# The first group's block in another order, with the second group's input products moved ahead of the first gate product

## The chip, the cores and the metric

The kernel runs on one core of a Trainium2 chip. The metric is the device time of one execution in microseconds (us); the median of several executions counts. TensorE (PE in the profile, PEld its weight loads), VectorE (DVE), ScalarE (ACT) and GpSimd (POOL) each work through their own instruction list in order; SyncE (SP) issues the DMAs. They meet only at semaphores: `then_inc` on the producer, `wait_ge` on the consumer.

## What is computed

Input: 2048 rows of 512 numbers (8 sequences of 256), float32.

```python
x = x + layernorm(attn(layernorm(x)))     # attn: rmsnorm -> mamba2 -> residual -> rmsnorm -> SwiGLU MLP
x = x + layernorm(ffn(layernorm(x)))      # ffn: linear 512x512 + LoRA of the one expert chosen by argmax
# mamba2(h), per sequence, chunks of 128:
z, xBC, dt = split(h @ w_in.T)            # 512 + 768 + 4 columns
xBC = silu(conv4(xBC) + conv_b); dt = softplus(dt + dt_bias)
Y = (att * exp-decay) @ (x*dt) + C @ state + D * xs
out = (Y * silu(z)) @ w_out.T
```

The SwiGLU MLP has an inner width of 1792, that is 14 blocks of 128.

## The kernel before

A **group** is one sequence (256 rows, two tiles of 128); there are 8. Each goes through three stages: A (both norms and mamba2), B (the MLP, 14 blocks f = 0..13) and C (the ffn). `steps` runs step t = 1..9 with A on group t, B on group t-1, C on group t-2. Within a step every engine has a hand-written table (`A_AT`, `NEXT_AT`, `C_AT`) that says after which block f it does which part of A and C. Group 0's stage A has no step to lie in: it is written out in a function `first()` of each engine. This is the head.

Matrices are multiplied as float16 pairs: each weight unit of 128 x 512 is split into an upper half (`upper_halves`, ACT, line 596) and a lower half (`lower_halves`, DVE, line 919), in place in the ring `W`: unit u is written where the raw of unit u-4 lay, so ACT waits for DVE's split of u-4. A product is then three matmuls for each pair of halves. The scale of the split comes from the largest norm of a matrix, for which PE multiplies every raw block by itself (`grams`, bf16), DVE takes the maximum and writes a diagonal (`prep_diag`), PE spreads it with a matmul (`spread`), and DVE makes the scale (`prep_scale`, `prep_inverse`). There are three such chains: 0 for w_in, 1 for gate and up, 2 for down and the ffn's linear. In the head units 0 to 9 (w_in), 10 to 17 (gate and up of f = 0..3) and 18 (down of f = 0) are split; the rest is split in step 1, three units ahead of each f, by `prepare(f)`, first on ACT, then on DVE.

Stage A, in the order of its data: `a_stats` (mean and variance, DVE), `a_norm` (powers, POOL), `a_center` and `a_hi1`/`a_lo1` (float16 pair of the normalised rows, DVE, ACT, DVE; group 0 uses `first_norm`), `a_t1` (transpose to `ht`: for group 0 on PE with ACT and DVE making the halves, for later groups two transposing DMAs), `a_in(g, b)` for three pairs of w_in units (24 matmuls each) and `a_z(g, b)` for two, `a_dt` (PE, then softplus on ACT with two table loads and ten small DVE operations), `a_conv` (ACT tap, three DVE passes of two operations), `a_silu`, `a_scan_in` and `a_tdt` (POOL, lines 468 and 476), `a_dec` (float32 products, exp on ACT, times dt on DVE), `a_tok` (transposes), `a_att`, `a_xd` (D times xs, POOL line 484, four operations), `a_xw`, `a_ce`, `a_state`, `a_y`, `a_o`, `a_h1`, then `a_sumsq`, `a_rms`, `first_h2`, `a_t2` (transpose of the second norm's rows to `h2t`). B needs `h2t`: `b_gu(g, f)` (gate and up, 24 matmuls), `b_silu`, `b_prod` (line 1092), `b_hi`, `b_lo` (line 1097), `b_down(g, f)` (line 1343, into `acc`), which comes one f later in PE's list.

For group 0 the convolution inputs of pairs 1 and 2 are copied to SBUF (`first_conv`, which is `h1b`), while pair 0 and all later groups convolve straight out of PSUM. `a_in(1, 0)` and `a_in(1, 1)` stand in step 1 at f = 0, behind `b_gu(0, 0)`. `centered` is the tile `dec` for every group, which is busy with group 0's decay until `a_y(0, 1)`; so group 1's rows are centered after that, split at the end of the head, and only then transposed by DMA. `a_in(1, b)` also waits until both `a_h1` of group 0 are done, since they read the banks.

## Time and profile before

| | |
|---|---|
| median of 3 runs | 805.33 us (804.77 to 807.54) |
| the profiled execution | 807.84 us, span 805.9 us |
| PE, DVE, ACT, POOL busy | 95%, 60%, 41%, 20% of the span |
| mean granted clock of PE | 0.976 |
| first gate product begins | 73.54 us |
| second group's first input product begins | 81.65 us |

The span runs from the first instruction to the last; the execution's time is 1.9 us more. Read the profile by the order of each engine's list: what an engine waited for stands in brackets behind the group of instructions that came after the wait. The granted clock is 1.00 at 2.4 GHz and 0.50 at 1.2 GHz; a PE that is "busy" at 0.50 does half the work.

### The profile page before, as it was taken

The numbers are of one execution on the slowest core, as the hardware profiler recorded it, in microseconds if no ns is written. First come the engines' busy times: TensorE is split into PE (matmuls) and PEld (weight loads), VectorE is DVE, ScalarE is ACT, GpSimd is POOL, SyncE is SP. The second block draws the span as 40 slices with busy tenths as digits, with TensorE's granted clock in tenths as the row PEclk, the third lists the DMA queues.
The fourth block names the chain that finished last, engine by engine and source line by source line (L and its number), as shares of the span: only waits on it lengthen the run. The fifth ranks groups of instructions, "written<-read, shape, count | busy, mean of one in ns | idle before, by whom it ended". The sixth has DMA issues, their size and how long they took to land.

```text
span 805.9 us, 13862 instructions
## 1 busy us (share of the span) xinstructions
PE 765.4 (95%) x5558; PEld 538.1 (67%) x5558; DVE 486.4 (60%) x1109; ACT 332.1 (41%) x603; POOL 157.6 (20%) x203
## 2 busy tenths in 40 slices
PE   3995989989999999999999999999999999999995
PEld 3863766668666876678666876678666876567752
DVE  6878576867744766447644766447644766246355
ACT  2753477445623364225623364235623354222221
POOL 1412131203301241103400141103400151001021
PEclk9897899999999999999999999999999999999997
DMA  9941000030202101040202101040202101021001
GB/s 319 387 174 22 6 27 1 1 79 2 54 0 53 54 27 27 5 101 2 53 1 53 53 27 28 0 106 1 54 1 53 54 1 27 1 79 27 28 0 53
DMA packets 59936, 41.11 MB, mean 51 GB/s; under 512 B 45664, under 2 KB 45792, under 8 KB 59872
## 3 DMA queue, kind: packets, MB, share of 16 engines
q1 hardware_dynamic: 59872, 40.22, 17.7%
q8 instruction: 44, 0.72, 0.4%
q14 instruction: 20, 0.16, 0.1%
HBM read 25.01 MB, written 4.19 MB: 36 GB/s over the span
## 4 chain that ended last, share of the span: by engine, by line
PE 88%; DVE 7%; DMA 2%; ACT 2%; issue 1%; SPq 1%; POOL 0%; ACTq 0%; DVEq 0%
PE gu L1343 35%; PE wa L1343 26%; PE acc L1343 20%; PE wc L1343 6%; DVE weights L919 1%; DMA weights<-in_w_in 1%; PE wa L1366 0%; DVE stats_a L1148 0%; DMA xa<-in_x 0%; DVE sg L1092 0%; DMA ht<-ra 0%; DVE act L1097 0%; PE wa L1431 0%; PE wc L1558 0%; ACT act L716 0%
## 5 line engine op out<-in xcount | busy, mean ns | idle before, releaser
L1343 PE MATMUL gu<-h2t,weights 128*128 128x256 f16 x2688 | 313.6, 274 | 0.6 <-DVE h2t L1086 0.6
L1343 PEld LDWEIGHTS gu<-h2t,weights 128*128 128x128 f16 x2688 | 261.3, 98 | 56.2 <-issue 19.3
L1343 PE MATMUL acc<-weights,act 128*128 128x512 f16 x672 | 164.6, 381 | 6.5 <-DVE act L1097 6.5
L1092 DVE SCALAR_TENSOR_TENSOR sg<-gu,bound,sg 128x256 f32<-128x256 f32 x112 | 53.5, 478 | 117.6 <-ACT sg L706 116.9
L706 ACT ACTIVATE sg<-gu,scale_inv 128x256 f32<-128x256 f32 x112 | 53.1, 474 | 161.8 <-PE gu L1343 161.6
L1343 PE MATMUL wa<-ht,weights 128*128 128x256 f16 x912 | 111.2, 281 | 3.4 <-DMA ht<-ra 3.4
L1343 PEld LDWEIGHTS acc<-weights,act 128*128 128x128 f16 x672 | 65.6, 98 | 64.2 <-DVE act L1097 8.3
L1343 PEld LDWEIGHTS wa<-ht,weights 128*128 128x128 f16 x912 | 91.9, 101 | 22.6 <-DMA ht<-ra 3.7
L1097 DVE TENSOR_TENSOR act<-sg,act 128x256 f16<-128x256 f32 x112 | 50.6, 452 | 54.1 <-ACT act L716 54.1
L716 ACT ACTIVATE act<-sg 128x256 f16<-128x256 f32 x112 | 46.6, 416 | 87.7 <-DVE sg L1092 87.7
L992 DVE SCALAR_TENSOR_TENSOR xbc<-wa,conv_ws,xbc 128x253 f32<-128x253 f32 (+1 forms) x132 | 57.3, 475 | 10.4 <-ACT xbc L633 8.9
L1343 PE MATMUL wa<-w_out_t,y 128*128 128x512 f32 x128 | 57.4, 592 | 0.0
L454 POOL TENSOR_SCALAR small_c<-mv_c 128x2 f32<-128x2 f32 x21 | 4.0, 193 | 223.8 <-DVE mv_c L936 223.8
L919 DVE SCALAR_TENSOR_TENSOR weights<-weights,scale_v 128x512 f16<-128x512 f32 x56 | 41.5, 796 | 7.0 <-ACT weights L596 6.9
L484 POOL TENSOR_SCALAR y<-xbc,rows_t 128x256 f32<-128x256 f32 x32 | 36.2, 1144 | 44.9 <-ACT xbc L644 44.9
L633 ACT ACTIVATE xbc<-wa,cols_t,conv_ws 128x256 f32<-128x256 f32 x48 | 24.5, 560 | 46.1 <-PE wa L1343 46.1
L1343 PEld LDWEIGHTS wa<-w_out_t,y 128*128 128x128 f32 x128 | 24.2, 190 | 25.5 <-issue 23.4
L454 POOL TENSOR_SCALAR small_a<-mv_a 128x2 f32<-128x2 f32 (+1 forms) x22 | 5.8, 261 | 160.6 <-DVE mv_a L936 106.0
L596 ACT ACTIVATE weights<-weights,scale_v 128x512 f16<-128x512 f32 x56 | 36.2, 710 | 0.5 <-DVE weights L919 0.4
L684 ACT ACTIVATE hn<-h 128x512 f32<-128x512 f32 x16 | 10.1, 631 | 62.3 <-DVE h L1060 62.3
L1343 PE MATMUL wc<-weights,h3t 128*128 128x512 f16 x144 | 33.0, 379 | 0.0
L468 POOL TENSOR_TENSOR ra<-tri,a_t 128x512 f32<-128x512 f32 x16 | 19.2, 1219 | 70.4 <-DVE a_t L1026 70.4
(208 smaller groups left out, 817.7 us busy)
## 6 DMA issues: line engine op xcount, KB each, us to landing
xa<-in_x SPq DMA_DIRECT2D x9, 512.0 KB, 3.5
weights<-in_x SPq DMA_DIRECT2D x7, 512.0 KB, 3.6
out_x<-h SPq DMA_DIRECT2D x14, 256.0 KB, 2.2
weights<-in_w_in SPq DMA_DIRECT2D x5, 512.0 KB, 7.2
weights<-in_w_down SPq DMA_DIRECT2D x3, 768.0 KB, 13.2
weights<-in_w_gate SPq DMA_DIRECT2D x2, 1024.0 KB, 12.2
weights<-in_w_up SPq DMA_DIRECT2D x2, 1024.0 KB, 13.8
weights<-in_w_gate SPq DMA_DIRECT2D x2, 768.0 KB, 14.0
```

The lines of the kernel that those rows point to most:

```text
L468: nc.gpsimd.tensor_tensor(ra[:, j], tri[:].unsqueeze(1).broadcast_to([P, H, P]), a_t[:, j].unsqueeze(2).broadcast_to([P, H, P]), ALU.mult)\
L484: nc.gpsimd.tensor_scalar(y[:, h], xbc[:, 0], rowt[:, 4 + h:5 + h], None, ALU.mult)\
L596: nc.scalar.activation(Wh[:, u, 0], W[:, u + SHIFT], ACT.Copy, scale=sv[:, t:t + 1])\
L633: nc.scalar.activation(xbc[:, c], src[:, m * SEQ:(m + 1) * SEQ], ACT.Identity, bias=conv_b[:, c:c + 1], scale=cw[:, c * TAPS + TAPS - 1:c ...
L684: nc.scalar.activation(hn[:, j], h01[:, j], ACT.Square, accum_out=ss[:, 0, j:j + 1])\
L706: nc.scalar.activation(sg[:, f % 2], GU[f % 2][:, 0:SEQ], ACT.Silu, scale=inv_gate)\
L716: nc.scalar.activation(act[:, slot(f), 0], sg[:, f % 2], ACT.Copy)\
L919: nc.vector.scalar_tensor_tensor(Wh[:, u, 1], W[:, u + SHIFT], sv[:, t:t + 1], Wh[:, u, 0], ALU.mult, ALU.subtract).then_inc(split, 1)
L992: ins = nc.vector.scalar_tensor_tensor(xbc[:, c, late:], conv_in(g, c)[:, 0:SEQ - late], cw[:, c * TAPS + k:c * TAPS + k + 1], xbc[:, c, l ...
L1092: nc.vector.scalar_tensor_tensor(sg[:, f % 2], GU[f % 2][:, SEQ:2 * SEQ], up_to_act, sg[:, f % 2], ALU.mult, ALU.mult).then_inc(sem("prod_ ...
L1097: nc.vector.tensor_tensor(act[:, slot(f), 1], sg[:, f % 2], act[:, slot(f), 0], ALU.subtract)\
L1343: return nc.tensor.matmul(dst, left, right, start=start, stop=stop)
```

## The change

Everything in it concerns the head and the first block of step 1.

1. **Loads.** The two norm rows are loaded apart (`ln1`, `ln2`), `dt` directly behind `ln1`, then w_in; the small rows and columns come behind w_in, `ln2` behind the first gate and up pieces. The second group's `xa` is issued behind the last up piece, ahead of w_out, instead of after all loads.
2. **PE.** The grams of the first gate and up pieces come right after `spread(0)`; `a_in(0, 0)` before `a_dt(0)`; `a_tok` after two of `a_dec`; `spread(1)` between `a_state` and `a_y(0, 1)` instead of before `a_z(0, 1)`; the grams of down and linear between `a_o(0, 0)` and `a_o(0, 1)`; `a_in(1, 0)` and `a_in(1, 1)` between `spread(2)` and `a_t2(0)`. `a_t2` uses the banks `GU` instead of `WA`.
3. **Centering.** Group 1 is centered in `hn`, so `a_stats(1)`, `a_center(1)` and `a_lo1(1)` lie beside group 0's attention, and `a_hi1(1)` right behind `a_state(0)`.
4. **DVE.** `a_h0(0)` goes to the start; `a_t1(0)` between `prep_diag(0)` and `prep_scale(0)`; `prep_inverse(0)` behind four lower halves; both late convolutions directly behind `a_dt(0)` and ahead of units 8 and 9; `ln_row(1)` behind `a_lo1(1)`; chain 1 beside `a_y`.
5. **ACT.** Four copies with a scale (`first_xd`) take the place of `a_xd(0)` on POOL; uppers 6 and 7 after the first tap, 8 and 9 after the last.

```diff
@@ sync
-            sp.dma_start(lnt[:].rearrange("p t d -> p (t d)"), ln_rows.broadcast_to([P, 2 * D]))\
-                .then_inc(small_loaded, 16)
-            sp.dma_start(colt[:], cols).then_inc(small_loaded, 16)
+            sp.dma_start(lnt[:, 0], ln_rows[:, 0:D].broadcast_to([P, D])).then_inc(ln1_loaded, 16)
+            sp.dma_start(dt_raw, w_dt).then_inc(dt_loaded, 16)
+            for n in IN:
+                load_piece(n)
             sp.dma_start(rowt[:], rows.broadcast_to([P, 16])).then_inc(small_loaded, 16)
-            sp.dma_start(dt_raw, w_dt).then_inc(small_loaded, 16)
-            for n in range(pieces_of(T_DOWN)[0]):
+            sp.dma_start(colt[:], cols).then_inc(small_loaded, 16)
+            load_piece(GATE[0])
+            load_piece(UP[0])
+            sp.dma_start(lnt[:, 1], ln_rows[:, D:2 * D].broadcast_to([P, D])).then_inc(ln2_loaded, 16)
+            for n in range(UP[0] + 1, DOWN[0]):
                 load_piece(n)
+            sp.wait_ge(sem("h0_ready"), 2)
+            sp.dma_start(xa[:], x_g[1]).then_inc(x_loaded, 16)
             sp.dma_start(wo[:], w_out.rearrange("k p n -> p k n")).then_inc(wo_loaded, 16)
...
-            a_x(1)
             a_t1(1)
             steps(step)
@@ shared
-        centered = dec[:].rearrange("p t h q -> p t (h q)")
+        def centered(g):
+            return hn if g == 1 else dec[:].rearrange("p t h q -> p t (h q)")
@@ scalar
+            def first_xd():
+                for h in range(H):
+                    nc.scalar.activation(y[:, h], xbc[:, 0], ACT.Copy, scale=rowt[:, 4 + h:5 + h])\
+                        .then_inc(sem("xd_ready"), 1)
...
                 small_hi(T_IN)
-                upper_halves(range(0, 9))
+                upper_halves(range(0, 6))
                 a_conv(0, 0)
-                upper_halves([9])
+                upper_halves(range(6, 8))
                 a_dt(0)
+                a_conv(0, 1)
                 a_silu(0, 0)
-                a_conv(0, 1)
                 a_conv(0, 2)
-                a_tok(0)
+                upper_halves(range(8, S_GU))
                 a_exp(0, 0)
                 a_exp(0, 1)
+                a_tok(0)
                 a_exp(0, 2)
...
                 a_z(0, 1)
+                first_xd()
+                a_state(0)
+                a_hi1(1)
                 upper_halves(range(S_GU, S_GU + 4))
@@ vector, first()
-                ln_row(1)
+                a_h0(0)
+                prep_diag(0)
                 a_t1(0)
-                prep_diag(0)
                 prep_scale(0)
...
-                lower_halves(range(0, 8))
+                lower_halves(range(4, 6))
                 a_dtv(0)
                 a_conv(0, 0)
+                lower_halves(range(6, 8))
                 a_dt(0)
+                a_conv(0, 1)
+                a_conv(0, 2)
                 lower_halves(range(8, S_GU))
-                a_conv(0, 1)
-                prep_diag(1)
-                a_conv(0, 2)
-                prep_scale(1)
                 a_dec(0, 0)
                 a_dec(0, 1)
+                a_stats(1)
                 a_att(0, 0)
                 a_att(0, 1)
+                a_center(1)
+                prep_diag(1)
+                a_y(0, 0)
+                prep_scale(1)
+                a_y(0, 1)
+                a_lo1(1)
+                dve.wait_ge(ln2_loaded, 16)
+                ln_row(1)
+                prep_inverse(1)
+                a_h1(0, 0)
                 lower_halves(range(S_GU, S_GU + 2))
...
                 prep_diag(2)
+                lower_halves(range(S_GU + 2, S_GU + 4))
                 a_h1(0, 1)
                 prep_scale(2)
                 prep_inverse(2)
+                lower_halves(range(S_GU + 4, S_GU + 5))
                 first_h2(0)
                 first_h2(1)
                 a_t2(0)
-                lower_halves(range(S_GU + 6, S_MIX))
-                a_lo1(1)
+                lower_halves(range(S_GU + 5, S_MIX))
@@ tensor
-            A_AT = {0: lambda g: (g == 1 and a_in(g, 0), a_in(g, 1)), 1: ...
+            A_AT = {0: lambda g: g > 1 and a_in(g, 1), 1: ...
...
                 spread(0)
+                grams(GATE[0], UP[0])
+                a_in(0, 0)
                 a_dt(0)
-                a_in(0, 0)
                 a_in(0, 1)
-                grams(GATE[0], UP[0])
                 a_in(0, 2)
-                grams(GATE[1], UP[1])
                 a_z(0, 0)
-                a_tok(0)
-                grams(GATE[2], UP[2], GATE[3], UP[3])
                 a_dec(0, 0)
                 a_dec(0, 1)
+                a_tok(0)
+                grams(GATE[1], UP[1])
                 a_dec(0, 2)
-                spread(1)
                 a_z(0, 1)
+                grams(GATE[2], UP[2])
                 a_att(0, 0)
                 a_att(0, 1)
-                grams(*DOWN)
+                grams(GATE[3], UP[3])
                 a_y(0, 0)
                 a_state(0)
+                spread(1)
                 a_y(0, 1)
-                grams(*LIN)
                 pe.wait_ge(wo_loaded, 16)
                 a_o(0, 0)
+                grams(*DOWN, *LIN)
                 a_o(0, 1)
                 spread(2)
+                a_in(1, 0)
+                a_in(1, 1)
                 a_t2(0)
```

## Rows read from the trace of the kernel before

**Rows 1.** Windows: us; PE, PEld, DVE, ACT, POOL busy; granted clock; DMA share.
```profile
74.25:115.30 41.05, 35.14 (x280) 27.62 (x278) 27.19 (x56) 21.77 (x39) 9.18 (x8) 0.87 0.07 14
115.30:168.00 52.70, 51.86 (x313) 34.26 (x313) 38.95 (x69) 34.17 (x61) 7.21 (x8) 0.97 0.15 33
200.00:300.00 100.00, 100.00 (x728) 70.77 (x727) 59.91 (x136) 42.39 (x77) 24.39 (x29) 1.00 0.15 38
```

**Rows 2.** Timeline 0 to 20: start, us, engine, line, operation [idle before].
```profile
6.83 0.69 DVE L828 TENSOR_REDUCE bound<-ln_rows_t 128x1 f32<-128x512 f32 x1 [0.82 <-DMA dt_raw<-in_w_dt]
...
14.08 1.48 DVE L974 TENSOR_TENSOR ht<-wa,ht 128x512 f16<-128x512 f32 x2 [0.74 <-ACT ht L609]
...
19.79 0.35 PE L1343 MATMUL wc<-dt_w,ht 128*128 128x4 f16 x8 [2.50 <-DVE dt_w L900]
```

**Rows 3.** DMA issues: the first up piece, us to landing.
```profile
weights<-in_w_up SPq DMA_DIRECT2D x1, 1024.0 KB, 12.3
```

**Rows 4.** Timeline 20 to 40: splits, products, POOL.
```profile
19.56 5.38 DVE L919 SCALAR_TENSOR_TENSOR weights<-weights,scale_v 128x512 f16<-128x512 f32 x8
...
20.45 8.21 PE L1343 MATMUL wa<-ht,weights 128*128 128x256 f16 x48
...
31.47 2.93 POOL L468 TENSOR_TENSOR ra<-tri,a_t 128x512 f32<-128x512 f32 x2 [23.22 <-DVE a_t L1026]
...
34.33 2.78 PE L1343 MATMUL gu<-ht,weights 128*128 128x256 f16 x24
34.36 2.39 POOL L476 TENSOR_TENSOR hn<-tri,dts 128x512 f32<-128x512 f32 x2
```

**Rows 5.** Timeline of DVE, 35.4 to 36.4: the convolution beside POOL.
```profile
34.60 2.43 DVE L992 SCALAR_TENSOR_TENSOR xbc<-h1b,conv_ws,xbc 128x253 f32<-128x253 f32 x2
```

**Rows 6.** Timeline 40 to 60: float32 products, a convolution, statistics.
```profile
40.49 1.93 PE L1343 MATMUL wa<-ra,below 128*128 128x512 f32 x4
...
41.48 2.70 DVE L992 SCALAR_TENSOR_TENSOR xbc<-h1b,conv_ws,xbc 128x253 f32<-128x253 f32 x6
...
58.64 1.29 DVE L934 BATCH_NORM_STATS2 stats_a<-xa 128x6 f32<-128x512 f32 x2 [0.91 <-DMA xa<-in_x]
```

**Rows 7.** Windows, DVE alone: four stretches of the head.
```profile
11.36:13.36 2.00, 1.81 (x6) 1.00 1.05 387
52.70:54.20 1.50, 1.43 (x3) 1.00 0.00 0
60.10:61.25 1.15, 0.98 (x7) 1.00 0.00 0
63.15:69.27 6.12, 5.46 (x20) 0.83 0.00 0
```

**Rows 8.** Timeline 60 to 80: from the second spread to the first gate product.
```profile
71.01 1.97 PE L1366 MATMUL wa<-ident,hn 128*128 128x128 f32 x8 [3.90 <-DVE hn L1066]
...
73.54 4.68 PE L1343 MATMUL gu<-h2t,weights 128*128 128x256 f16 x24 [0.56 <-DVE h2t L1086]
...
76.23 1.41 DVE L981 SCALAR_TENSOR_TENSOR ra<-dec,small_a,ra 128x512 f16<-128x512 f32 x2
```

**Rows 9.** Timeline 78 to 100: the second group's first input products.
```profile
81.65 8.34 PE L1343 MATMUL wa<-ht,weights 128*128 128x256 f16 x48 [3.43 <-DMA ht<-ra]
```

**Rows 10.** Timeline 100 to 135: the stall of the first step.
```profile
109.45 3.63 DVE L919 SCALAR_TENSOR_TENSOR weights<-weights,scale_v 128x512 f16<-128x512 f32 x3
...
113.96 1.30 DVE L1097 TENSOR_TENSOR act<-sg,act 128x256 f16<-128x256 f32 x1 [0.48 <-ACT act L716]
...
115.32 2.74 PE L1343 MATMUL acc<-weights,act 128*128 128x512 f16 x6 [2.50 <-DVE act L1097]
```

**Rows 11.** Windows of 1 us: the granted clock after idle time.
```profile
115.00:116.00 1.00, 0.68 (x2) 0.28 (x3) 1.00 (x3) 1.00 (x3) 0.00 (x0) 0.50 0.00 0
118.00:119.00 1.00, 1.00 (x6) 0.76 (x5) 0.56 (x2) 0.41 (x2) 0.00 (x0) 0.80 0.90 332
168.00:169.00 1.00, 0.18 (x1) 0.11 (x2) 0.66 (x2) 0.67 (x2) 0.00 (x0) 1.00 0.69 264
```

More of the change, by code:

```diff
@@ L361, in _ @@
             sp.dma_start(lora_raw, lora_b).then_inc(lora_loaded, 16)
-            for n in range(pieces_of(T_DOWN)[0], len(PIECES)):
+            for n in range(DOWN[0], len(PIECES)):
                 load_piece(n)
@@ L480, in a_xd @@
             def a_xd(g):
-                prev(g, 2, 2, pool, sem("o_ps_ready"))
+                pool.wait_ge(sem("o_ps_ready"), g * 2)
                 pool.wait_ge(sem("xbc_ready"), g * 3 + 1)
@@ L565, in first @@
                 a_tdt(0)
-                a_xd(0)
                 a_xw(0)
@@ L616, in a_hi1 @@
                     eng.wait_ge(sem("centered"), g * 2 + j + 1)
-                    nc.scalar.activation(rows_1[:, j, 0], centered[:, j], ACT.Copy, scale=s_a[:, 1, j:j + 1])\
+                    nc.scalar.activation(rows_1[:, j, 0], centered(g)[:, j], ACT.Copy, scale=s_a[:, 1, j:j + 1])\
                         .then_inc(sem("hn_hi"), 1)
@@ L623, in a_conv @@
                 src = in_bank(b)
+                if head(g) and b == 0:
+                    eng.wait_ge(sem("taps_scaled"), 1)
                 if b == 0:
@@ L780, in first @@
                 chain_a.group(0)
+                a_t1(0)
                 prep_a()
-                a_t1(0)
                 small_hi(T_IN)
-                upper_halves(range(0, 9))
+                upper_halves(range(0, 6))
                 a_conv(0, 0)
-                upper_halves([9])
+                upper_halves(range(6, 8))
                 a_dt(0)
+                a_conv(0, 1)
                 a_silu(0, 0)
-                a_conv(0, 1)
                 a_conv(0, 2)
-                a_tok(0)
+                upper_halves(range(8, S_GU))
                 a_exp(0, 0)
                 a_exp(0, 1)
+                a_tok(0)
                 a_exp(0, 2)
@@ L798, in first @@
                 a_z(0, 1)
+                first_xd()
+                a_state(0)
+                a_hi1(1)
                 upper_halves(range(S_GU, S_GU + 4))
-                a_state(0)
-                upper_halves(range(S_GU + 4, S_GU + 7))
                 a_sumsq(0, 0)
+                upper_halves(range(S_GU + 4, S_GU + 5))
                 a_sumsq(0, 1)
-                upper_halves(range(S_GU + 7, S_MIX))
+                upper_halves(range(S_GU + 5, S_GU + 8))
                 a_t2(0)
-                a_hi1(1)
+                upper_halves(range(S_GU + 8, S_MIX))
                 chain_a.close()
@@ L1287, in first @@
                 a_stats(0)
-                dve.wait_ge(small_loaded, 64)
+                dve.wait_ge(ln1_loaded, 16)
                 ln_row(0)
                 first_norm()
+                dve.wait_ge(dt_loaded, 16)
                 small_max(dt_raw, 0)
-                ln_row(1)
+                a_h0(0)
+                prep_diag(0)
                 a_t1(0)
-                prep_diag(0)
                 prep_scale(0)
                 prep_small(T_IN, 0)
+                lower_halves(range(0, 2))
+                prep_small(T_IN, 1)
+                lower_halves(range(2, 4))
+                dve.wait_ge(small_loaded, 32)
                 prep_inverse(0)
-                prep_small(T_IN, 1)
-                lower_halves(range(0, 8))
+                lower_halves(range(4, 6))
                 a_dtv(0)
                 a_conv(0, 0)
+                lower_halves(range(6, 8))
                 a_dt(0)
+                a_conv(0, 1)
+                a_conv(0, 2)
                 lower_halves(range(8, S_GU))
-                a_conv(0, 1)
-                prep_diag(1)
-                a_conv(0, 2)
-                prep_scale(1)
                 a_dec(0, 0)
                 a_dec(0, 1)
+                a_stats(1)
                 a_att(0, 0)
                 a_att(0, 1)
-                lower_halves(range(S_GU, S_GU + 2))
-                a_y(0, 0)
-                a_h0(0)
-                lower_halves(range(S_GU + 2, S_GU + 4))
-                a_y(0, 1)
-                a_stats(1)
-                prep_inverse(1)
-                lower_halves(range(S_GU + 4, S_GU + 6))
-                a_h1(0, 0)
-                a_center(1)
+                a_center(1)
[8 more added lines that the diff above has]
+                a_h1(0, 0)
+                lower_halves(range(S_GU, S_GU + 2))
                 dve.wait_ge(lora_loaded, 32)
@@ L1490, in a_t2 @@
                 for b in range(2):
-                    transposed(hn, WA[b], b, sem("h2t_ps_ready"))
+                    transposed(hn, GU[b], b, sem("h2t_ps_ready"))
             def b_gu(g, f):
@@ L1593, in last @@
                     c_lora(LAST, j)
-            A_AT = {0: lambda g: (g == 1 and a_in(g, 0), a_in(g, 1)), 1: lambda g: (a_in(g, 2), a_dt(g)), 2: lambda g: a_z(g, 0),
+            A_AT = {0: lambda g: g > 1 and a_in(g, 1), 1: lambda g: (a_in(g, 2), a_dt(g)), 2: lambda g: a_z(g, 0),
                     3: lambda g: a_z(g, 1), 4: lambda g: (a_tok(g), a_dec(g, 0), a_dec(g, 1)),
```

16 lines of the change are left out of this document (9 added, 7 removed).

## The prediction

> **What bounds the kernel.** I read the windows first. From 200 us on PE has no idle time at all and runs at full clock; VectorE is busy 60%, ScalarE 42% [rows 1]. The change touches nothing there, so whatever is won or lost before PE has become the bound is carried to the end one for one. Between the first split and step 1's stall PE is busy for 35.1 of 41.05 us, at a mean clock of 0.87, and from 115.3 to 168 for 51.9 of 52.7 us [rows 1]. So the event to follow is `b_down(0, 3)`, which begins at 115.32 after a wait of 2.5 us for `b_lo` [rows 10]: behind it PE is the bound, VectorE (38.95 of 52.7 us) is not. I call it S. The forecast is 805.33 less what S moves, corrected for the clock.
>
> I then read the timeline of the head for PE's waits: 2.5 us before `a_dt(0)` [rows 2], 3.9 us before `a_t2` [rows 8], 3.43 us for `ht` before `a_in(1, 0)` [rows 9], 2.5 us at S [rows 10]. Clock: a full-rate product of 24 matmuls takes 2.78 us with its drain [rows 4], 2.62 us from start to start; the first gate product took 4.68 [rows 8], the first 48 matmuls of group 1 took 8.34 [rows 9] and those of group 0 8.21 [rows 4], so each of the three ran largely at 1.2 GHz. After the 2.5 us wait the clock was 0.50 in 115 to 116 and came back in 118 to 119; after 1.6 us of idle time in 167 to 169 it had stayed at 1.00 [rows 10, 11]. The change attacks the waits at 71.0 and 81.65 and their slow products.
>
> **Up to the first split: nothing.** VectorE waited until 6.83 for the last small load, 0.82 us [rows 2]; now it needs `ln1` only, and w_in lands earlier, behind 0.28 MB less. That makes the rows and grams 0.8 us earlier. But `a_t1(0)`, 1.48 us that lay in the wait for the grams [rows 2], now stands between `prep_diag(0)` and `prep_scale(0)`, where only PE's `spread` (0.5 us) covers it. I take the scale, and the first product at 20.5, as unchanged (bounds: 0.8 us earlier, 0.5 later). `a_h0(0)` (1.0 us) fits before the grams. The first up piece landed 12.3 us after an issue at 7.3, so at 19.6 [rows 3]; now 0.7 to 1.2 us earlier, and its grams (1.8 us with gate's) fill the old 2.5 us wait. The breaks in PE are then near 1 us each, so I take full clock for the first products.
>
> **20.5 to 41: the split of units 8 and 9.** At 0.67 us per unit [rows 4], with `prep_inverse(0)` (0.9) after unit 3, VectorE has unit 5 at 25.0, `a_conv(0, 0)` at 27.9, units 6 and 7 at 29.3, and `a_dt` at 31.3. So POOL starts at 31.4, as before (31.47), and works to 36.7: 2.93 and 2.39 us [rows 4]. PE: four pairs and `a_dt` to 31.7, `a_dec` when POOL has its halves (32.9, 34.3), `a_tok`, six units of grams, `a_dec(0, 2)`, done at 37.8. Then `a_z(0, 1)` needs the lower half of unit 8, which now comes after both late convolutions. These read two SBUF tiles. Alone their six operations take 2.70 us, 0.45 each [rows 6]; beside POOL two took 2.43 us, 1.22 each [rows 5]. In POOL's 5.3 us 4.4 of the 12 get done, the other 7.6 take 3.4 us: 40.1. Unit 8 follows at 40.8, unit 9 at 41.5. PE waits 3.0 us. The Trainium skill has a rule that speaks against this place (SBUF — State Buffer, "Who interferes with whom"): a DVE instruction with two SBUF inputs contends with a GpSimd instruction that reads SBUF. By it both late convolutions stand behind POOL, the 3.0 us gap opens, and the sum ends at 799; were there no such contention, it would end at 793.
>
> **41 to the first gate product, at full clock.** `a_z(0, 1)` ends at 43.4. A unit of grams is 0.23 us, a float32 product of 512 columns 0.86 (two took 1.93 with the drain [rows 6]). Eight units of grams to 45.2, `a_att` to 47.0, six units to 48.4, `a_y(0, 0)` and `a_state` to 50.1, while VectorE does `a_att(0, 1)` at 47.7, `a_center` (1.4) 49.1 and `prep_diag(1)` 50.25, so `spread(1)` waits 0.2 and `a_y(0, 1)` ends at 52.8. `a_stats(1)` (1.3 [rows 6] and 0.3) lies in the wait for `a_att`. Now VectorE is full: `a_y(0, 0)` 1.4 [rows 7], `prep_scale(1)` 1.25, `a_y(0, 1)` 1.4, `a_lo1` 1.4 [rows 8], `ln_row(1)` 2.0 and `prep_inverse(1)` 1.1 [rows 7] with `a_h1(0, 0)` 0.7, two units 1.4, `small_max` 0.5, `prep_diag(2)` 1.35, two units 1.4: from 50.25 to 64.2. PE's `a_o(0, 0)` 3.45, 18 units of grams 4.1 and `a_o(0, 1)` 3.45 end at 63.9: the two are level. `a_h1(0, 1)` is done at 65.0, and with it `a_in(1, 0)` may start; `ht` has long landed (`a_lo1` ends at 55.8; before, it took 4.0 us from there to 81.65). Both pairs end at 70.2. Meanwhile VectorE does `prep_scale(2)` to `first_h2` (in part in the 6.1 us stretch of [rows 7]): h2 at 69.4. So the wait for h2 is filled, and nothing is late in its place. `a_t2` and its halves take 2.5 us (71.01 to 73.54 [rows 8]): the first gate product at 72.7, where it was at 73.54. ScalarE's `first_xd` is four operations of 0.5 us from 42 on; ScalarE next has `a_state` at 50, so it costs nothing; if it had no cover, 2 us. What it takes off POOL was 4 us, behind which nothing waits.
>
> **The clock in that gap.** PE has 3.0 us idle before `a_z(0, 1)`, behind gaps of 1.2 and 0.6. Waits of 2.5 us or more were each followed by half clock, those of 1.6 were not [rows 2, 9, 10, 11]. It came back 3.1 us after the restart [rows 11] or, in `a_in(0)` and `a_in(1)`, only after most of their time: 8.34 less 5.24 is 3.1 us lost, 8.21 less 5.24 is 3.0 [rows 4, 9]. So a fall costs 1.5 to 3.1 us; I take 2.5, because `a_z` and `a_att` stand in the way of everything behind. The first gate product is then at 75.2, 1.7 us later than before.
>
> **To S.** From there VectorE sets the pace. Before, it was busy 27.2 us from 74.25 to S [rows 1], and idle the rest, most of it for `ht`. After: 27.2 less `a_lo1` 1.4 [rows 8], plus one lower half 0.7 and 0.6 for two lower halves beside POOL's `a_xd(1)` (0.96 for 0.67); plus the waits it cannot avoid: four times ScalarE's 0.45 between product and lower half, 0.6 for the first tap, 1.3 for softplus with its two table loads, and some 0.9 where `prepare` waits for ScalarE, which begins with splits of its own. 31.7 us from the end of `a_t2`'s last half, which is 0.7 us behind the first gate product, so S is 32.4 to 32.8 us behind it; I take 32.7. The stretch of [rows 10] is in it unchanged: 3.63 us for three lower halves and 1.30 for `b_lo` beside POOL. S: 75.2 + 32.7 = 107.9, against 115.32: 7.4 us earlier. So of the 17 us that PE's list wins (3.4 for `ht`, 3.9 for h2, the slow halves of three products), VectorE in step 1 takes back most; PE now waits some 5 us at S instead of 2.5. That longer wait makes 0 to 1.6 us more at half clock; I take 1.0. Gain 6.4 us. The profiled execution goes from 807.84 to 801.4 (span 799.5); the median of the runs, 2.5 us under it, from 805.33 to 798.9, rounded 799.0.
>
> **The rivals.** *The clock holds in the gap.* S is at 72.7 + 32.7 = 105.4, the gain 9.9 less 1.0: 796.5. For it: the gap is a difference of two long sums and may come out at 2 us. Against: all four waits of 2.5 us or more saw a fall. *The convolutions don't slow down beside POOL* (POOL yields, or is later). They end at 36.7, unit 8 is there at 37.4, no gap: the first gate product at 69.7, S at 102.4, less 1.0: 793.4. Against: [rows 5]. *The step takes more back.* If the halves of each f in step 1 also wait for ScalarE (it has 21.8 us of work to S [rows 1], and the step begins 10 us sooner for it), 1 us in each of f = 0..3 is lost: 803.0, at the edge of no difference. *Slower.* One mechanism: the clock, once down at 41, stays down, because the short float32 products with their waits in the attention don't keep it up. Every us of PE work at half rate costs half a us; it turns the sign when the 6.4 us are eaten, that is 12.8 us of half rate beyond the 5 that I count, until about 59. If it is down until `a_in(1, 0)` starts near 67, some 18 us beyond the 5 count, with PE on the path for all of them: 798.9 + 9 = 808. Against: the longest half-rate stretch before with work in it was about 6 us. *The products don't fill the wait*: `ht` lands after 65. It is issued 9 us before that and takes 4; then they would delay h2 and gain nothing, 804 to 806.
>
> **How the numbers follow.** The clock falls in the gap (my forecast) 0.52, it holds 0.18, no slow-down beside POOL 0.07, the step takes more back 0.11, the clock stays down 0.06, the products miss the wait 0.03, better than all of these 0.03. A half clock for the first products (from 20.5 on, as before) would add 1.2 us to any of them, since POOL starts that much later. The forecast's own range is 797 to 801.5. The range of eight in ten, 794.0 to 803.8, leaves out the last two bad cases and most of the best. A change of 0.3% is 2.4 us, about what this measurement can tell from none: 802.9 to 807.7 is "same". Faster: 0.49 of the forecast, 0.18, 0.07, 0.05, 0.03 makes 0.82; same 0.03, 0.05, 0.02, 0.02 makes 0.12; slower 0.06.
>
> **What would show it.** `a_z(0, 1)` starts near 41 after 3 us idle, clock 0.5 behind it. `a_in(1, 0)` starts near 67 without waiting for `ht`, and `a_t2` within 1 us of its end. First gate product near 75. S near 108 with about 5 us of idle time before it, released by `b_lo`; VectorE with almost no idle time from the first gate product to it. From S on the trace is the old one, shifted. It would be wrong above all if VectorE's convolutions run otherwise beside POOL, or if the idle time at S is much above 5 us.

## The result, and the profile after

The changed kernel takes 796.6 us (median of 5 runs, 792.34 to 797.88), the kernel before 805.76 on the same occasions (804.77 to 807.54). The ratio is 0.9873, with a 95% interval of 0.9854 to 0.9891: 1.3% faster. The forecast was 799.0 with a range of 794.0 to 803.8.

The profiled execution of the changed kernel is its fastest one, 792.34 us, span 790.6, mean granted clock 0.992. A second profiled execution, in the run called `again` below, took 795.9 us, span 794.2, clock 0.988, and is nearer to the median. They are called the first and the second profile, and both are shown, since what tells them apart is one of the results. G is the start of the first gate product, S the start of `b_down(0, 3)`, as in the prediction.

The first profile: the head up to `a_z(0, 1)`, which answers to [rows 4, 5]; then PE around the first gate product, to [rows 8, 9]; then the stall at S, to [rows 10].

```profile
20.37 2.78 PE L1368 MATMUL wa<-ht,weights 128*128 128x256 f16 x24
...
30.06 8.20 DVE L1011 SCALAR_TENSOR_TENSOR xbc<-h1b,conv_ws,xbc 128x253 f32<-128x253 f32 x12
30.22 2.40 POOL L477 TENSOR_TENSOR ra<-tri,a_t 128x512 f32<-128x512 f32 x2 [21.75 <-DVE a_t L1045]
...
38.98 2.79 PE L1368 MATMUL gu<-ht,weights 128*128 128x256 f16 x24 [2.51 <-DVE weights L938]
```
```profile
63.18 5.40 PE L1368 MATMUL wa<-ht,weights 128*128 128x256 f16 x48 [0.44 <-DVE h L1079]
...
68.42 1.04 PE L1391 MATMUL gu<-ident,hn 128*128 128x128 f32 x8
...
70.43 5.41 PE L1368 MATMUL gu<-h2t,weights 128*128 128x256 f16 x48 [0.98 <-DVE h2t L1105]
```
```profile
95.22 3.64 DVE L938 SCALAR_TENSOR_TENSOR weights<-weights,scale_v 128x512 f16<-128x512 f32 x3
...
99.74 1.30 DVE L1116 TENSOR_TENSOR act<-sg,act 128x256 f16<-128x256 f32 x1 [0.48 <-ACT act L731]
...
101.09 1.47 PE L1368 MATMUL acc<-weights,act 128*128 128x512 f16 x6 [3.75 <-DVE act L1116]
```

`a_in(1, 0)` and `a_in(1, 1)` stand ahead of `a_t2` and take 5.40 us where they took 8.34 [rows 9]; the wait of 3.9 us for h2 and the one of 3.43 for `ht` are gone, 0.98 is left; the first two gate products, 5.41 us together, run without a break and at full clock. The stall S in front of `b_down(0, 3)` has grown from 2.50 to 3.75 us [rows 10], and 3.64 and 1.30 us of VectorE beside POOL stand in front of it unchanged. `a_z(0, 1)` waits 2.51 us for VectorE. S is at 101.09 instead of 115.32. In this execution the clock is 1.00 from the first matmul to the end of `b_down(0, 3)`.

The same places in the second profile, PE only, and the clock around them (windows as in [rows 1]):

```profile
17.72 1.89 PE L1368 MATMUL acc<-weights 128*128 128x128 bf16 x16 [2.25 <-DMA weights<-in_w_gate]
...
20.43 1.89 PE L1368 MATMUL acc<-weights 128*128 128x128 bf16 x16 [0.82 <-DMA weights<-in_w_up]
...
22.11 3.50 PE L1368 MATMUL wa<-ht,weights 128*128 128x256 f16 x24
```
```profile
41.44 2.79 PE L1368 MATMUL gu<-ht,weights 128*128 128x256 f16 x24 [2.50 <-DVE weights L938]
```
```profile
103.55 2.74 PE L1368 MATMUL acc<-weights,act 128*128 128x512 f16 x6 [3.74 <-DVE act L1116]
...
109.53 2.78 PE L1368 MATMUL gu<-h2t,weights 128*128 128x256 f16 x24
```
```profile
17.00:18.00 1.00, 0.28 (x3) 0.29 (x4) 0.30 (x2) 0.63 (x2) 0.00 (x0) 0.50 1.05 399
20.00:21.00 1.00, 0.57 (x6) 0.58 (x7) 1.00 (x3) 1.00 (x3) 0.00 (x0) 0.50 1.07 391
41.00:42.00 1.00, 0.56 (x6) 0.50 (x6) 1.00 (x3) 1.00 (x3) 0.00 (x0) 1.00 1.05 389
102.00:103.00 1.00, 0.00 (x0) 0.00 (x0) 0.81 (x1) 1.00 (x3) 1.00 (x2) 0.55 0.00 0
105.00:106.00 1.00, 1.00 (x4) 0.38 (x2) 1.00 (x3) 0.45 (x2) 0.00 (x0) 0.50 0.60 49
```

PE waits 2.25 us for the first gate piece and 0.82 for the first up piece to land; the clock falls there, not in front of `a_z(0, 1)`, where it is 1.00 in 41 to 42, at the end of a wait of 2.50 us; and it falls again at S. From S to the next gate product it is 5.98 us, where it was 4.85 in the kernel before (115.32 [rows 10] to 120.17) and is 3.35 in the first profile, which has no half clock there. `a_in(0, 0)` starts 1.7 us later than in the first profile, and S is at 103.55, 11.8 us before the old one. The spans differ by 11.7 (805.9 and 794.2).

The 1.1 us more at S come back in the last 20 us of the span, where 18 matmuls into `acc`, at half clock for a part, take 5.23 us and took 6.35 before. The first profile has 6.00 there. What comes between is fixed: from the first output product `a_o` behind S to this last group it is 647.7 us in the kernel before and in both profiles. So the clock at the end of the span varies as well, by 1.1 us here, and no run shows why. The kernel before (its next gate product first), then the second profile:

```profile
120.17 2.78 PE L1343 MATMUL gu<-h2t,weights 128*128 128x256 f16 x24
...
789.56 6.35 PE L1343 MATMUL acc<-weights,h3t 128*128 128x512 f16 x18
```
```profile
778.92 5.23 PE L1368 MATMUL acc<-weights,h3t 128*128 128x512 f16 x18
```

### The profile page after: what moved, and what is told of

It reads as the page before. It is cut to its first block, busy times and chain, and to the rows that moved or that the text cites. A ratio compares the mean times of both kernels' runs of the same rounds, so it can differ in the third digit from the quotient of the medians.

```text
span 790.6 us, 13864 instructions
## 1 busy us (share of the span) xinstructions
PE 755.6 (96%) x5558; PEld 532.0 (67%) x5558; DVE 485.1 (61%) x1109; ACT 332.5 (42%) x607; POOL 152.7 (19%) x199
## 4 chain that ended last, share of the span: by engine, by line
PE 84%; DVE 10%; ACT 2%; issue 1%; DMA 1%; POOL 0%; SPq 0%; ACTq 0%; DVEq 0%
PE gu L1368 34%; PE wa L1368 24%; PE acc L1368 19%; PE wc L1368 6%; DVE weights L938 3%; DVE xbc L1011 2%; DMA weights<-in_w_in 1%; DVE sg L1111 1%; DVE stats_a L1167 0%; ACT act L731 0%; ACT weights L604 0%; PE wc L1583 0%; DVE hn L1173 0%; DVE act L1116 0%; PE wa L1456 0%
## 5 line engine op out<-in xcount | busy, mean ns | idle before, releaser
L1368 PE MATMUL wa<-ht,weights 128*128 128x256 f16 x912 | 105.4, 273 | 0.4 <-DVE h L1079 0.4
L1368 PEld LDWEIGHTS wa<-ht,weights 128*128 128x128 f16 x912 | 89.0, 98 | 16.8 <-issue 0.8
L493 POOL TENSOR_SCALAR y<-xbc,rows_t 128x256 f32<-128x256 f32 x28 | 32.8, 1186 | 35.1 <-ACT xbc L654 35.1
L1079 DVE TENSOR_TENSOR h<-wa,h 128x512 f32<-128x512 f32 x16 | 11.1, 691 | 35.4 <-PE wa L1368 35.3
```

What stands on the lines that cost most here:

```text
L493: nc.gpsimd.tensor_scalar(y[:, h], xbc[:, 0], rowt[:, 4 + h:5 + h], None, ALU.mult)\
L1079: nc.vector.tensor_tensor(h01[:, j], o_bank(g, j)[:], h01[:, j], ALU.add)\
L1368: return nc.tensor.matmul(dst, left, right, start=start, stop=stop)
```

## The experiments

Twelve runs followed the first one, `again` being the changed kernel once more. All but pool_later were measured four to six times beside the kernel before on the same chip, and are compared by that ratio; the times are those of one profiled execution each. S - G is the time from G to S.

| run | median us | ratio (95%) | `a_z(0, 1)` starts, takes | G | S - G |
|---|---|---|---|---|---|
| changed kernel | 796.6 | 0.9873 (0.9854 to 0.9891) | 38.98, 2.79 | 70.43 | 30.66 |
| again | 796.4 | 0.9880 (0.9865 to 0.9895) | 41.44, 2.79 | 72.89 | 30.66 |
| fill_gap | 795.9 | 0.9871 (0.9855 to 0.9888) | 42.88, 2.79 | 74.32 | 30.66 |
| gap_wide | 801.2 | 0.9940 (0.9924 to 0.9956) | 45.16, 5.30 | 79.39 | 30.65 |
| pairs_back | 800.2 | 0.9922 (0.9908 to 0.9936) | 42.74, 2.79 | 74.04 | 34.42 |
| fill_early | 794.2 | 0.9856 (0.9837 to 0.9875) | 40.38, 2.79 | 71.83 | 30.67 |
| up_later | 797.3 | 0.9877 (0.9855 to 0.9900) | 42.33, 4.46 | 75.45 | 30.66 |
| prepare_last | 796.2 | 0.9881 (0.9864 to 0.9899) | 43.70, 4.46 | 76.81 | 26.42 |
| split_first | 793.1 | 0.9846 (0.9825 to 0.9867) | 39.35, 2.79 | 70.93 | 30.67 |
| center_dec | 798.7 | 0.9905 (0.9889 to 0.9921) | 42.25, 4.46 | 76.54 | 30.67 |
| xd_on_pool | 798.4 | 0.9907 (0.9891 to 0.9922) | 42.89, 2.79 | 74.33 | 30.66 |
| pool_later | 802.6 (one run) | | 48.86, 2.78 | 80.30 | 30.66 |
| split_fill | 790.3 | 0.9801 (0.9783 to 0.9818) | 36.91, 2.79 | 68.48 | 30.66 |

**again.** The changed kernel, unaltered.

> The changed kernel once more, as the yardstick for the others of this chip and to see how its executions spread. Theory: the executions differ by whether PE's clock falls in the 2.5 us gap before a_z(0, 1) and in the 3.7 us stall in front of b_down(0, 3). Those at a mean clock of 0.992 take about 792 us, those at 0.988 about 796 (0.4% of 795 us at half rate is 6.4 us longer at half clock, 3.2 us of time). Rival: the spread has nothing to do with the clock, and time and mean clock are unrelated.

Four more executions, 795.9 to 797.4, all at 0.988. With the first five (792.34 at 0.992, 794.7 at 0.990, 796.6 to 797.9 at 0.988) time follows the clock. From 0.992 to 0.988 it is 3.6 to 5.5 us where 3.2 were expected, and within 0.988 it is still 2 us, so the clock is not all of the spread. In the kernel before it is the same: of eleven executions beside this run two took 804.2 and 805.3 us at 0.984 and six 806.3 to 807.3 at 0.976. Of the two places named, the second profile shows one (S) and not the other. Its G is 2.46 us later than in the first profile: the first up piece landed 1.0 us later (20.43 and 19.43), and half clock costs 0.7 us in that piece's grams and 0.7 in `a_in(0, 0)`.

**fill_gap**, on PE in front of `a_z(0, 1)`; the result is in no one's way and is not read:

```diff
+                for _ in range(40):
+                    mm(GU[1][:, 0:P], upper(ident[:]), upper(ident[:]), True, True)
                 a_z(0, 1)
```

> 40 matmuls of 128 columns, whose result nobody reads, are put on PE in front of a_z(0, 1), where it waits for VectorE; they take about 2.3 us of a gap of 2.5. Nothing else is changed. Theory (the clock sometimes falls in the gap): the executions gather near 792 to 794, the median 1 to 3 us under the changed kernel's. Rival (the gap has no part in the spread, only the later stall has): the same median and the same spread as the changed kernel.

0.9871 against 0.9873 and 0.9880: no difference, and 795.7 to 797.3 us instead of 792 to 794. My own theory of the gap fell here. Its profile has the fall in front of `a_in(0, 0)`, which takes 4.55 us.

**gap_wide.** VectorE's halves of units 8 and 9 come later.

```diff
                 a_conv(0, 2)
-                lower_halves(range(8, S_GU))
...
                 a_stats(1)
+                lower_halves(range(8, S_GU))
```

> The lower halves of units 8 and 9 come three DVE steps later still, behind a_dec(0, 0), a_dec(0, 1) and a_stats(1): the gap in front of a_z(0, 1) grows from 2.5 to about 5.5 us. Theory: PE is on the path there, everything behind shifts by some 2 to 3 us, and the clock now falls in the gap in every execution, 2 to 3 us more: 797 to 800 in all executions. Rival (the gap has slack behind it, since VectorE is full from the attention on): within 1 us of the changed kernel.

```profile
45.16 5.30 PE L1368 MATMUL gu<-ht,weights 128*128 128x256 f16 x24 [6.04 <-DVE weights L938]
```

The gap is 6.0 us now, and `a_z(0, 1)` takes 5.30 us at half clock instead of 2.79. Its start moved 3.7 us against the second profile, G 6.5, the time 4.8 (801.2 against 796.4), just above the 797 to 800 expected. So PE is on the path there, and behind a wait that long the clock did fall, for 2.5 us on the product alone: the price that I had put on a fall. The 2.5 us of idle time brought none about in either profile of the changed kernel.

**pairs_back.** The matmuls of `a_in(1, 0)` and `a_in(1, 1)` go back to f = 0 of step 1.

```diff
-            A_AT = {0: lambda g: g > 1 and a_in(g, 1), 1: lambda g: (a_in(g, 2), a_dt(g)), 2: lambda g: a_z(g, 0),
+            A_AT = {0: lambda g: (g == 1 and a_in(g, 0), a_in(g, 1)), 1: lambda g: (a_in(g, 2), a_dt(g)), 2: lambda g: a_z(g, 0),
...
                 spread(2)
-                a_in(1, 0)
-                a_in(1, 1)
                 a_t2(0)
```

> a_in(1, 0) and a_in(1, 1) go back into step 1 behind b_gu(0, 0); all else of the change stays. Theory (VectorE sets the pace of step 1 up to b_down(0, 3)): the first gate product comes where h2 allows, about 0.5 us earlier at full clock, and b_down(0, 3) starts at most 1 to 2 us later than in the changed kernel, so 0 to 2 us slower, plus what the clock costs, since PE then stands idle for 5 us before a_t2: 1 to 3 us. In all 1 to 5 us slower. Rival (PE sets the pace): the whole 5.2 us of both pairs are lost, plus the clock, 6 to 8 us slower.

```profile
71.51 1.97 PE L1391 MATMUL gu<-ident,hn 128*128 128x128 f32 x8 [5.02 <-DVE hn L1085]
74.04 3.85 PE L1368 MATMUL gu<-h2t,weights 128*128 128x256 f16 x24 [0.56 <-DVE h2t L1105]
77.73 5.40 PE L1368 MATMUL wa<-ht,weights 128*128 128x256 f16 x48
```
```profile
108.46 1.47 PE L1368 MATMUL acc<-weights,act 128*128 128x512 f16 x6 [2.50 <-DVE act L1116]
```

3.8 us slower than `again`, and from the start of `a_z(0, 1)` to S it is 65.7 us instead of 62.1, 3.6 more. PE waits for h2 and comes out of it at half clock: from `a_t2` to the first gate product 2.53 us instead of 2.01, from that to the next product 3.69 instead of 2.62. These are 1.6 us more of half clock. If they delay S in full, the other 2.0 are what 5.2 us of matmuls are worth in step 1; that split is a subtraction, and no run separates the two. Ahead of G the pairs had cost nothing, since they lay in the wait for h2. From G to S PE is busy 31.92 us instead of 25.80 and waits 2.50 instead of 4.87 (1.12 and 3.75), so its waits pay for 2.4 us of the 6.1. VectorE alone doesn't set the pace any more: its waits for ScalarE grow, for softplus from 1.21 to 2.38 us, because ScalarE now waits for PE's products.

The rest of the gain can be read here too. S - G was 41.78 us in the kernel before (73.54 to 115.32) and is 34.42 here, with the pairs at the old place. These 7.4 us are the 3.43 us that PE no longer waits for `ht`, and 3.9 us less PE time for the same 282 matmuls (35.85 and 31.92 busy), at a clock of 0.97 instead of 0.87. What brings `ht` early, the loads or the split in the head, was not taken apart, except for the centering (center_dec).

**fill_early** puts unread matmuls into PE's waits behind `spread(0)`:

```diff
                 spread(0)
-                grams(GATE[0], UP[0])
+                for _ in range(36):
+                    mm(GU[0][:, 0:P], upper(ident[:]), upper(ident[:]), True, True)
+                grams(GATE[0])
+                for _ in range(16):
+                    mm(GU[0][:, 0:P], upper(ident[:]), upper(ident[:]), True, True)
+                grams(UP[0])
```

> Matmuls whose result nobody reads fill PE's waits behind spread(0): 36 of them (2 us) before the grams of the first gate piece and 16 (0.9 us) before those of the first up piece. In the second look at the changed kernel the clock fell there (at 16.9 us, after a wait of 2.25 us for the gate piece) and not before a_z(0, 1). Theory: with them the clock holds in the head, a_in(0, 0) takes 2.6 us instead of 3.5, and the median falls to 793 to 795. Rival (the executions of about 796 come from the fall in front of b_down(0, 3) alone): no difference.

```profile
16.35 2.23 PE L1368 MATMUL gu<-ident 128*128 128x128 bf16 x36
...
19.33 1.08 PE L1368 MATMUL gu<-ident 128*128 128x128 bf16 x16
...
21.77 2.78 PE L1368 MATMUL wa<-ht,weights 128*128 128x256 f16 x24
```

`a_in(0, 0)` takes 2.78 us where the second profile had 3.50, and the clock is 1.00 up to S. 794.2 us, at mean clocks of 0.990 to 0.994, where seven of nine executions of the changed kernel had 0.988. The ratios' intervals overlap, so the 2 us alone would be weak. The profiles say the same: of the eleven without these matmuls ten have half clock between 16 and 27 us, of the two with them none has.

**up_later.** The grams of the first up piece stand behind the first product.

```diff
-                grams(GATE[0], UP[0])
+                grams(GATE[0])
                 a_in(0, 0)
+                grams(UP[0])
```

> The grams of the first up piece move behind a_in(0, 0). In the second look at the changed kernel the chain runs from the landing of that piece at 20.4 through its grams into a_in(0, 0) at 22.1, and on through a_conv(0, 0) into everything that VectorE does; the scale was there at 17.3. Theory: a_in(0, 0) now starts at 19 to 20, up to 2 us earlier than in that look, and as VectorE is full from there on the end follows: 1 to 2 us faster than the changed kernel. Rival (the gap before a_z(0, 1) takes it up, or the fallen clock takes it back): no difference.

```profile
20.49 5.28 PE L1368 MATMUL wa<-ht,weights 128*128 128x256 f16 x24 [1.89 <-DVE weights L938]
```

No difference (0.9877). `a_in(0, 0)` starts at 20.49, a little behind the 19 to 20 expected, after 1.89 us of waiting for the split, and runs at half clock, 5.28 us. What the earlier start gave, the clock took: the rival. In this profile the clock fell a second time, in the gap before `a_z(0, 1)` (4.46 us for it).

**prepare_last.** In step 1 the splits stand behind `b_silu`, `b_hi` on ScalarE and, with the same edit, behind `b_prod`, `b_lo` on VectorE.

```diff
-                    if a == 1:
-                        prepare(f)
                     if b is not None:
...
                         b_lo(b, f)
+                    if a == 1:
+                        prepare(f)
```

> In step 1 ScalarE and VectorE do the three splits of each f behind b_silu, b_hi and b_prod, b_lo instead of ahead of them. Same work. Theory (the stall in front of b_down(0, 3) is b_lo waiting behind the splits, 3.64 us of them slowed by POOL): b_lo(0, 3) is done some 3 us earlier, the 3.7 us stall shrinks to under 1 us, the clock does not fall there (1.5 us more): 3 to 5 us faster than the changed kernel. Rival (VectorE as a whole is the bound, its sum is unchanged): the stall moves to a later f, less than 1 us faster.

```profile
103.23 1.47 PE L1368 MATMUL acc<-weights,act 128*128 128x512 f16 x6 [0.80 <-DVE act L1116]
...
115.70 0.49 DVE L1111 SCALAR_TENSOR_TENSOR sg<-gu,bound,sg 128x256 f32<-128x256 f32 x1 [3.70 <-ACT sg L721]
...
121.94 1.45 PE L1368 MATMUL wa<-hn,tok 128*128 128x512 f32 x2 [2.46 <-POOL hn L500]
123.18 4.15 PE L1368 MATMUL gu<-h2t,weights 128*128 128x256 f16 x24
```

The wait at S is 0.80 us and S - G 26.42, 4.2 us less, yet the time is the same. PE now waits elsewhere: POOL's `a_xw` comes late, 2.46 us at 121.94, and the gate product behind that takes 4.15 us instead of 2.78, at half clock. From G to the gate product behind the second `a_o` it is 68.95 us here and 67.25 in the first profile. 1.7 us of half clock at that place (1.4 in the product, 0.3 in the one ahead of it) are the difference; the waits come to 4.7 us here and 5.0 there. The executions' clocks are 0.984 to 0.986, so some of the time is clock too. The rival holds in its result: the stall moved and the time did not. Its reason, VectorE's sum, isn't shown. VectorE is busy 30.3 of the 42.5 us behind S, and at 115.70 it waits 3.70 us for ScalarE, which works without a break from 108.86 to there (a `b_hi`, three splits, exp, two table loads, a `b_silu`). Both engines' lists are on the path in turn. This profile also began late and lost the clock twice in the head, which is why its G is 76.8; the stall's move does not depend on that.

**split_first.** VectorE:

```diff
                 a_conv(0, 1)
-                a_conv(0, 2)
                 lower_halves(range(8, S_GU))
+                a_conv(0, 2)
```

> The lower halves of units 8 and 9 come between the two late convolutions (ScalarE's order is unchanged). Theory: a_z(0, 1) no longer waits 2.5 us; a_att comes 1.4 to 1.8 us earlier, limited now by VectorE's own sum; the end follows by 1 to 1.8 us. Rival (VectorE's sum decides, not the place of the two units): 0 to 0.5 us.

793.1 us, 0.9846: 2 to 3 us faster. In this profile `a_in(0, 0)` started 0.4 us later than in `again`, `a_z(0, 1)` 2.1 us earlier, G 2.0 earlier. `a_z(0, 1)` doesn't wait any more. It moved as expected, and a little more than its size, though the interval overlaps the changed kernel's at its edge.

**center_dec.** Group 1 is centered in `dec`, so later.

```diff
-            return hn if g == 1 else dec[:].rearrange("p t h q -> p t (h q)")
+            return dec[:].rearrange("p t h q -> p t (h q)")
...
-                a_center(1)
                 prep_diag(1)
...
-                a_lo1(1)
+                a_center(1)
                 dve.wait_ge(ln2_loaded, 16)
                 ln_row(1)
+                a_lo1(1)
```

> Group 1 is centered in dec again, so a_center(1) comes behind a_y(0, 1) and a_lo1(1) behind ln_row(1). Same work. In the changed kernel ht has landed by about 57.5, 5 us before a_in(1, 0) can start at 63.2, which waits for a_h1(0, 1). Theory: VectorE has nothing to do for 1.8 us before a_att(0, 0), so the 1.4 us of centering now fall behind instead of beside; prep_diag(1) and a_y(0, 0) come 1.4 us earlier for it. Since PE is level there, 0 to 1.5 us slower; ht does not become the wait. Rival (the early centering is what makes the pairs possible): PE waits for ht, 2 us or more slower.

```profile
69.29 5.40 PE L1368 MATMUL wa<-ht,weights 128*128 128x256 f16 x48 [1.32 <-DVE h L1079]
```

2.3 us slower, more than expected. PE waits 1.32 us for `a_h1(0, 1)` instead of 0.44, and never for `ht`. From the end of `a_z(0, 1)` to `a_in(1, 0)` it is some 1.2 us longer. The other us I put down to the clock, which fell in the gap in this profile and was 0.984 in four of six executions; that is argued. Centering early is worth VectorE's idle time, not an earlier `ht`.

**xd_on_pool** and **pool_later** are about the slow convolutions: one gives `first_xd` back to POOL, the other makes POOL wait for the convolutions.

```diff
-                pool.wait_ge(sem("o_ps_ready"), g * 2)
+                prev(g, 2, 2, pool, sem("o_ps_ready"))
...
                 a_tdt(0)
+                a_xd(0)
...
-                first_xd()
```

```diff
                 pool.wait_ge(sem("a_ready"), g + 1)
+                if head(g):
+                    pool.wait_ge(sem("conv_ready"), XBC)
```

> a_xd(0) goes back to POOL, behind a_tdt(0), and first_xd is gone from ScalarE. Same work. Theory (POOL slows a DVE operation that reads two SBUF tiles): POOL is busy for 4 us more from 35.0, which covers the last seven operations of the late convolutions, 0.70 us each instead of 0.45: a_z(0, 1) waits 3.5 to 4.5 us instead of 2.5, the end 1 to 2 us later. Rival (no slow-down from this kind of POOL operation, or the gap is hidden): within 0.5 us.

> A look at the disputed price: POOL starts the scan only when the late convolutions are done (one wait more on POOL). Theory (POOL is what makes them slow): the twelve operations take 5.4 us instead of 8.2, units 8 and 9 are there before 37, but a_dec(0, 0) must wait for POOL until about 37, so the whole gets slower by 1 to 3 us. Rival (they are slow because their input lies in SBUF): still 8 us.

```profile
33.08 9.09 DVE L1011 SCALAR_TENSOR_TENSOR xbc<-h1b,conv_ws,xbc 128x253 f32<-128x253 f32 x12
```
```profile
42.89 2.79 PE L1368 MATMUL gu<-ht,weights 128*128 128x256 f16 x24 [3.39 <-DVE weights L938]
```
```profile
34.66 5.32 DVE L1013 SCALAR_TENSOR_TENSOR xbc<-h1b,conv_ws,xbc 128x253 f32<-128x253 f32 x12
```

With POOL quiet the twelve operations take 5.32 us, in the changed kernel 8.20, with four more POOL operations behind them 9.09. So POOL is what makes them slow, by 2.9 us, though their input lies in the same place. The rule of the Trainium skill weighed in the prediction (SBUF — State Buffer, "Who interferes with whom"), that a DVE instruction with two SBUF inputs contends with a GpSimd instruction that reads SBUF, agrees with these three times.

In xd_on_pool the wait before `a_z(0, 1)` is 3.39 us instead of 2.51, just under the 3.5 to 4.5 expected, and the time is up by 2.0 us. pool_later has one execution only, 802.6 us, 6 above the second profile and not the 1 to 3 expected. G is 7.4 us later: the scan starts at 40.1, and the clock is 0.50 from 41 to 47, in PE's wait for it and behind; that fall I had not counted.

**split_fill.** The edits of split_first and fill_early, and unread matmuls in front of `b_down(0, 3)`:

```diff
                         b_gu(b, f)
+                        if b == 0 and f == 4:
+                            pe.wait_ge(sem("dtv_ready"), 2)
+                            for _ in range(60):
+                                mm(WC[:, 0:P], upper(ident[:]), upper(ident[:]), True, True)
```

The wait lets VectorE read `dt` out of that tile first.

> The two things that helped, and the clock's other place: the lower halves of units 8 and 9 between the late convolutions; the unread matmuls behind spread(0); and 60 more of them (3.4 us) in front of b_down(0, 3), where PE waits 3.7 us for VectorE. Theory (what is left above VectorE's sequence is half clock): every execution at a mean clock of 0.994 or more, the median 789 to 792, 1 to 3 us under split_first, with a smaller spread. Rival (the fill only moves the low stretch, or delays the matmuls behind it): as split_first, 793.

```profile
99.14 1.47 PE L1368 MATMUL acc<-weights,act 128*128 128x512 f16 x6 [0.31 <-DVE act L1116]
```
```profile
98.00:99.00 1.00, 0.84 (x15) 0.66 (x12) 1.00 (x1) 1.00 (x3) 0.80 (x1) 1.00 0.00 0
103.00:104.00 1.00, 1.00 (x11) 0.90 (x10) 0.29 (x1) 0.98 (x2) 0.00 (x0) 1.00 0.14 53
```

790.3 us (789.18 to 791.25), 2% under the kernel before and 0.7% under the changed one. The clock is 1.00 on both sides of S; three of four executions are at 0.996, the fourth, which is the profiled one, at 0.992, below the 0.994 expected. Over split_first it only adds matmuls that nobody reads, and is 2.8 us faster.

Nearly all of that comes from the head. The spans of the two profiles also differ by 2.8 us (788.6 and 791.4), and 2.46 of them are there at S (99.14 and 101.60): `a_in(0, 0)` starts 1.63 us earlier, 0.86 of it because the up piece landed earlier, and takes 0.82 us less. The fill at S does what it should on the spot, 3.36 us to the next gate product instead of 5.04. Yet from S to the end of the span it is 689.5 us against 689.8. Of the 1.7 us some 0.7 are gone by the first `a_o` behind S (25.79 and 26.74 us), and 0.6 in the last group of 18 matmuls (5.90 and 5.28 us). The other profiles agree: S to the end is 689.5 to 689.6 us in the two others without half clock behind S and with the same list from there (first, pairs_back), and 689.5 to 689.8 in the four others that lose 1.7 us there (fill_early, center_dec, xd_on_pool, pool_later). The remaining four come to 690.5 to 691.0, fill_gap among them, which loses 1.5 us at S and has 6.34 in the last group, so the two places don't always balance. For the fill at S the rival holds in this pair of profiles, to 0.3 us: the low stretch moved. Why the last group is slower when S was not is open.

## Why the prediction was right, and where not

- *Behind S nothing changes.* Right in the sum, 11.8 us at S and 11.7 in the span of the second profile, but made of 1.1 us lost right behind S and 1.1 won in the last group of matmuls, both clock, which cancel by luck.
- *Up to the first split: nothing.* Right in the first profile (20.37 against 20.45), too good for the usual execution: the twelve other profiles have it between 20.5 and 23.3. The grams put in front of `a_in(0, 0)` wait for their pieces, and the clock falls in these waits. I had the first up piece landing late and saw no harm in it.
- *The convolutions beside POOL and the gap.* Right: 8.20 us against 8.8, a gap of 2.51 against 3.0; pool_later shows the cause. `a_z(0, 1)` starts at 38.98 in the first profile, 41.44 in the second, for 40.8: the splits were done 1.2 us before I had them, and in the second profile the late start took that back.
- *The clock falls in the gap, 2.5 us.* This step failed, for the changed kernel. Neither profile shows it, and fill_gap, which removes the gap's idle time, gains nothing. In the second profile it falls in front of `a_in(0, 0)` instead, for 1.5 us (3.50 for 2.78 in the product, 1.89 for 1.09 in the first up piece's grams). The fall is possible in the gap (up_later, prepare_last and center_dec show one, gap_wide with 6 us of idle time too), but the same 2.5 us passed without one in four profiles (the first, `again`, fill_early, pairs_back), and 3.39 in xd_on_pool. Where it fell behind 2.5 us it cost 1.7 us up to S (63.78 from `a_z(0, 1)` in up_later, 62.11 in `again`), not 2.5, so the price was too high as well. What came true is the rival *the clock holds in the gap*, which I had given a chance of 0.18. From the start of `a_z(0, 1)` to the first gate product I had 31.9 us at full clock; it is 31.45.
- *S - G, 32.7 us.* VectorE sets the pace: right for this order, since from the last half of `a_t2` (70.97) to S it is busy 25.97 of 30.12 us and the rest is its waits for ScalarE, 3.6 us, and the breaks between operations. The size was off: 30.66 in every profile with this order. The 2.0 us too much are these. VectorE's work was 27.1 in my sum, 1.1 too much: the 27.2 of [rows 1] already held three splits slowed by `a_xd(1)`, 2.54 us, so my 0.6 for that counted them twice, and they now took 2.20. Its waits were 4.6, 0.45 too much: the 0.9 for `prepare` waiting for ScalarE isn't in the trace (VectorE did seven splits in 4.72 us), while those for ScalarE's product (four of 0.48), softplus (1.2) and the tap (0.5) are. The last half of `a_t2` ended 0.54 us behind G and not 0.7, and 0.3 is what I had added to my own 32.4.
- *1.0 us more half clock at S.* Right in the second profile, 1.1. In the first profile there is none at all, 1.5 less than before. What half clock at S costs in the end is less than it costs on the spot (split_fill).

The sum, for the second profile: I had S at 107.9, it is at 103.55. Of these 4.35 us 2.5 are the fall in the gap, 2.0 are S - G and 0.45 the stretch from the gap to G, less 0.64 for the later start of `a_z(0, 1)`. With the 1.1 us won back at the end that makes about 5.5: 801.4 forecast for a profiled execution, 795.9 measured. The median is off by 2.4 only (799.0 and 796.6), because I took the median 2.5 us under the profiled execution, as before; the changed kernel's second profile lies 0.5 under the median of its run. The old profiled execution had a clock of 0.976, the lowest of those that the kernel before shows, so those 2.5 us were in the main clock as well. That the forecast came this near is luck in part: 6.4 us of gain were forecast and 9.2 measured in the median. The rival that came true had 796.5 against 796.6, also with luck: it had S at 105.4, which is 1.85 us late.

## What to carry to other kernels

Moving matmuls into a wait pays what the engines that set the pace let through, not their duration: 3.6 us from `a_z(0, 1)` to S for 5.2 us moved, of which up to 1.6 are clock. Price a wait of PE twice, by its length and by the half clock behind it, and profile several executions before naming the place, since the same 2.5 us wait had both outcomes. Unread matmuls in PE's waits show in one run what the clock costs, but follow the effect to the end of the span: in the head they were worth some 2 us, at S 1.7 on the spot and 0.3 at the end.

## What the runs showed of the hardware

- Where the granted clock falls moves from execution to execution of the same program: nine executions of the changed kernel had mean clocks of 0.988 to 0.992 and took 792.3 to 797.9 us, and of its two profiles one has half clock behind waits of 2.25, 0.82 and 3.74 us, the other has waits of 0.42, 1.61 and 3.75 us at the same places and no half clock behind any.
- The loads land at different times in kernels with the same loads. PE began on the first w_in piece between 7.4 and 9.7 us of the span. What delayed `a_in(0, 0)` was the first up piece: where PE waited for it, it came between 19.4 and 21.6 us. The second profile had the earliest first piece (7.39) and yet a late start (22.11). This is a second source of spread, as large as one fall.
- With unread 128-column matmuls in PE's waits (36 of them take 2.23 us) the clock stayed at 1.00 behind those waits. In fill_early PE still waited 0.43 us for the up piece behind them, and in split_fill 0.31 us for `b_lo` at S, so there they delayed nothing. In the head of split_fill no wait is left, and a small cost is not excluded.
